# Moving a scan's multiplier into PSUM, sharing two accumulator banks, and moving a norm into the scan

## What is computed

```
delta = softplus(x_trans @ W1 + b1)                  # 128 channels per token
Bm, Cm = x_trans @ W2 + b2, x_trans @ W3 + b3        # 16 states per token
dA    = exp(-celu(delta[..., None] * A))             # A is 128 x 16
h_new = dA * h_prev + x_trans[..., None] * delta[..., None] * Bm
output = einsum('bln,bldn->bld', Cm, h_new)          # summed over the 16 states
```

## Time and profile before

| | us |
|---|---|
| median of 3 runs | 293.52 |
| the 3 runs | 293.46, 293.52, 296.5 |
| the profiled execution | 293.67 |
| its span | 292.0 |
| PE, DVE, ACT, POOL busy | 234.0, 249.1, 178.7, 137.4 |

### The profile page before, as it was taken

The page is one execution under the profiler, slowest core; times in us unless marked ns, Lnnn a source line. Parts: engine busy times, 40 slices in busy tenths (PEclk is TensorE's granted clock), DMA queues, the critical chain, the costliest instruction groups (busy, mean ns, idle before and its releaser), DMA issues.

```text
span 292.0 us, 2594 instructions
## 1 busy us (share of the span) xinstructions
PE 234.0 (80%) x825; PEld 152.2 (52%) x825; DVE 249.1 (85%) x358; ACT 178.7 (61%) x234; POOL 137.4 (47%) x89
## 2 busy tenths in 40 slices
PE   0837767987997476985997887959899999999980
PEld 0836435633664143442453343417688877888860
DVE  4996999999998999999999998578995459799465
ACT  3566874669779967687697875275533365083320
POOL 2360795000006246999778974203873328435310
PEclk9977999999999659799898997999999999999997
DMA  6920000000000000000000000000000000020002
GB/s 181 396 97 1 3 0 0 0 0 0 2 0 0 0 0 1 0 0 3 0 0 0 0 1 0 0 2 2 0 2 0 0 0 3 0 72 2 0 0 72
DMA packets 3822, 6.15 MB, mean 21 GB/s; under 512 B 384, under 2 KB 2656, under 8 KB 3552
## 3 DMA queue, kind: packets, MB, share of 16 engines
q1 hardware_dynamic: 3808, 5.97, 6.0%
HBM read 4.92 MB, written 1.05 MB: 20 GB/s over the span
## 4 chain that ended last, share of the span: by engine, by line
DVE 48%; PE 38%; issue 8%; ACT 3%; DMA 1%; DVEq 0%; ACTq 0%
PE ps L1084 12%; PE ps L1085 12%; DVE bs L804 6%; DVE bx L804 4%; DVE bs L798 4%; PE ps L1036 4%; PE ps L1055 3%; DVE x1r L725 3%; DVE bx L798 3%; DVE bs L835 2%; PE ps L935 2%; DVE tr L725 2%; DVE xr L850 2%; DVE x1r L723 2%; DVE low_max L714 1%
## 5 line engine op out<-in xcount | busy, mean ns | idle before, releaser
L577 ACT ACTIVATE bs<-ps,vec 128x512 f32<-128x512 f32 x48 | 32.5, 690 | 37.2 <-PE ps L1085 36.0
L1036 PE MATMUL ps<-tr,h0sel 96*128 96x512 f32 x64 | 22.7, 479 | 13.0 <-DVE bx L804 7.1
L1055 PE MATMUL ps<-bs,centre 128*128 128x512 f32 x52 | 28.5, 689 | 0.0
L396 POOL TENSOR_TENSOR xr<-bs,xr 128x512 fp32r<-128x512 f32 x12 | 15.9, 1331 | 26.7 <-DVE xr L850 26.7
L354 POOL TENSOR_TENSOR bdl<-bs 128x512 f32<-128x512 f32 x4 | 5.1, 1282 | 47.2 <-DVE bs L771 47.2
L1036 PEld LDWEIGHTS ps<-tr,h0sel 96*128 96x128 f32 x64 | 12.2, 206 | 28.1 <-DVE bs L804 13.4
L1084 PE MATMUL ps<-xr,wf 128*128 128x512 f32 x64 | 25.2, 393 | 0.0
L798 DVE SCALAR_TENSOR_TENSOR bs<-bdl,amax,bs 128x1024 f32<-128x1024 f32 x14 | 25.1, 1825 | 0.0
L1085 PE MATMUL ps<-xr,wf 128*128 128x512 f32 x64 | 25.1, 391 | 0.0
L545 ACT ACTIVATE bs<-bs 128x2048 f32<-128x2048 f32 x9 | 17.2, 1906 | 9.7 <-DVE bs L798 7.0
L804 DVE TENSOR_TENSOR bs<-bs,ps 128x2048 f32<-128x2048 f32 x9 | 20.5, 2280 | 0.9 <-PE ps L1036 0.9
(11 more groups left out here) (219 smaller groups left out, 682.2 us busy)
## 6 DMA issues: line engine op xcount, KB each, us to landing
bs<-in_w_mlp_dram SPq DMA_DIRECT2D x2, 1024.0 KB, 9.6
bx<-in_x_dram SPq DMA_DIRECT2D x4, 256.0 KB, 4.6
out_dram<-bdl SPq DMA_DIRECT2D x4, 256.0 KB, 2.3
bx<-in_w_mlp_dram SPq DMA_DIRECT2D x1, 768.0 KB, 6.7
bdl<-in_w_ssm_dram SPq DMA_DIRECT2D x1, 448.0 KB, 9.3
wa<-in_w_attn_dram SPq DMA_DIRECT2D x1, 256.0 KB, 2.8
w0raw<-in_w_ffn_dram SPq DMA_DIRECT2D x1, 192.0 KB, 8.6
h0T<-in_state_dram SPq DMA_DIRECT2D x1, 48.0 KB, 8.8
```

What stands on the lines that cost most here:

```text
L396: g.tensor_tensor(sl[:, 1, o, :], hbuf[k][:, o, :], full(sl[:, 0, o, :]), ALU.subtract).then_inc(m_lo_p, 1)
L577: a.activation(hbuf[k][:, o, :], ps[:, mbank(i, stage, k, o) % RING, :], ACT.Gelu if stage else ACT.Silu, scale=vec[:, s + o:s + o + 1]).t ...
L1036: last = m.matmul(ps[:, 2 * j + k, :], h0sel[:, n, :], tr[0:96, 0, cs(2 * (e // NG) + k)], start=True, stop=True)
L1055: last = m.matmul(ps[:, 4 + 2 * (e // NG) + k, :], centre[:, :], vbuf[e % NB][:, j, k * CH:(k + 1) * CH], start=False, stop=(e % NG == NG ...
```

## The change

What it does:

1. delta of the running pair is kept also in PSUM banks 6 and 7 (`delta_ps`), and `state_v` reads it there. DVE writes it for the first pair with two sums of 128 x 512, and for the second pair with one copy of 128 x 1024 in pass 7.
2. Both pairs accumulate in banks 4 and 5. The second pair's `state_first` waits for the first pair's norm, so the sums of passes 8 to 11 are taken later than before; the buffers are 7 instead of 5 for that (two more lie in the unused tile of the x splits). The feed-forward layer's ring of banks becomes 0, 1, 2, 3, 6, 7.
3. The first pair's norm is inside the scan: squares and copies in pass 10, variance in pass 10, ln and exp in pass 11, products and splits in passes 12 and 13. The second pair's stays behind the scan, with three tiles of the feed-forward layer's products ahead of its variance.
4. The beginning: ACT moves C and B out of PSUM unrounded (`c_and_b`), POOL rounds C and takes its low part (`c_parts`), DVE copies B and multiplies (`c_times_b`), DVE instead of POOL adds up delta of the first pair, the exponents of pass 0 come ahead of the logarithms of chunks 2 and 3.
5. POOL takes one `state_v` in passes 3, 5, 6, 7, 9, 10, 11, 13 and 14 (9, before 7).

```diff
-        vbuf = [b[:, :].rearrange("p (k n) -> p k n", k=GN) for b in (bx1, bx2, bs1, bs2, bs3)]
+        vbuf = [b.rearrange("p (k n) -> p k n", k=GN)
+                for b in (bx1[:, :], bx2[:, :], x1_f32[:, 0, 2:], x1_f32[:, 1, 2:], bs1[:, :],
+                          bs2[:, :], bs3[:, :])]
+        D_BANK = (6, 7, 4, 5)
+        delta_ps = ps[:, 6:8, :]
...
-            return e % 2 == 1 and e > 1 and j == 1
+            return e % 4 != 0 and 2 < e < NE - 1 and j == 1
...
+            def c_parts(c):
+                pool.wait_ge(c_full, c + 1)
+                g.tensor_copy(tr[0:96, 0, cs(c)], bs3[0:96, cs(c)]).then_inc(c_hi, 1)
+                pool.wait_ge(c_hi, c + 1)
+                g.tensor_tensor(tr[32:64, 0, cs(c)], bs3[32:64, cs(c)], full(tr[32:64, 0, cs(c)]),
+                                ALU.subtract).then_inc(c_lo, 1)
...
+            c_parts(0)
+            c_parts(1)
+            pool.wait_ge(d_ok0, 2)
+            gain_of(0)
+            gain_of(1)
+            c_parts(2)
+            c_parts(3)
...
             for e in range(NE):
                 if e + 1 < NE:
                     state_t(e + 1)
                 state_da(e)
+                if e < 2:
+                    log_part(2 + e)
                 if e == NG + 2:
+                    y3_square(0)
+                    y3_square(1)
+                if e == NG + 3:
+                    y3_rstd(0)
+                    y3_rstd(1)
...
+                        tile = vbuf[e % NB][:, j, :].rearrange("p (k n) -> p k n", n=CH)
+                        v.scalar_tensor_tensor(tile, delta_ps, amax[:, n:n + 1], tile, ALU.mult,
+                                               ALU.add).then_inc(e_v, 1)
...
+            def x3(c):
+                dve.wait_ge(y3_rs, c + 1)
+                v.tensor_tensor(bxt[:, cs(c)], bxt[:, cs(c)], bdl[:, cs(c)], ALU.mult).then_inc(x3_ok, 1)
+                split(x3_ok, x3_hi, x3_lo, bxt, lambda c: parts(lr, c), c)
...
             for e in range(NE):
+                if e + 1 == NG:
+                    delta_of_second_pair()
                 if e + 1 < NE:
                     state_v(e + 1)
                 state_p(e)
                 if e in (0, 1):
-                    direct(2 + e)
+                    direct(2 * e)
+                    direct(2 * e + 1)
+                if e == NG + 2:
+                    y3_copy(0)
+                    y3_copy(1)
+                if e in (NG + 4, NG + 5):
+                    x3(e - NG - 4)
...
+                if 1 <= e <= NG or e > NG + 4:
                     state_sum(e - 1)
+                if e == NG + 2:
+                    y3_variance(0)
+                    y3_variance(1)
+                if e == NG + 3:
+                    state_first(2)
+                    state_first(3)
+                    state_sum(NG)
+                    state_sum(NG + 1)
+                if e == NG + 4:
+                    state_sum(NG + 2)
+                    state_sum(NG + 3)
```

More of the change, by code:

```diff
@@ L237, in build, with ring @@
         PAIR = 6 * KH
-        RING = 6
+        RING_BANKS = (0, 1, 2, 3, 6, 7)
+        RING = len(RING_BANKS)
+        OUT_BANK = 4
+        def ring(b):
+            return ps[:, RING_BANKS[b % RING], :]
         def mtile(i, stage, k, o):
@@ L373, in _ @@
             r = 0
-            for e in range(1, NE, 2):
+            for e in range(1, NE):
                 if r < len(on_pool) and on_pool[r][0] == e:
@@ L552, in _ @@
                 state_da(e)
+                if e < 2:
+                    log_part(2 + e)
                 if e == NG + 2:
[L554 to L562, removed]
+                    y3_square(0)
[3 more added lines that the diff above has]
+                    y3_rstd(1)
+            y3_square(2)
+            y3_square(3)
+            y3_rstd(2)
+            y3_rstd(3)
             def norm_sd(i, k):
@@ L824, in _ @@
             v.tensor_tensor(b[:, 0, :], b[:, 0, :], b[:, 1, :], ALU.add).then_inc(e_add_last, 1)
-            for c in range(NCH):
-                dve.wait_ge(y3_rs, c + 1)
-                v.tensor_tensor(bx2[:, cs(c)], ps[:, 4 + c, :], bx2[:, cs(c)], ALU.mult).then_inc(x3_ok, 1)
-                split(x3_ok, x3_hi, x3_lo, bx2, lambda c: parts(lr, c), c)
+            y3_copy(2)
+            y3_copy(3)
+            x3(2)
+            x3(3)
             def mlp_tiles(i, stage, k):
@@ L1017, in _ @@
             pe.wait_ge(f1_ok, NCH)
-            m.matmul(ps[:, 7, 0:NLOW], ones[:, :], low_max[:, :], start=True, stop=True).then_inc(low_mm, 1)
+            m.matmul(ps[:, 5, 0:NLOW], ones[:, :], low_max[:, :], start=True, stop=True).then_inc(low_mm, 1)
             for c in range(NCH):
@@ L1088, in product, with gated @@
                 return last
-            def gated(low_weights, i, k):
+            def gated(low_weights, i, k, tiles):
                 wait_split(pe, x3_lo, 2 * i + k)
-                for o in range(KH):
+                for o in tiles:
                     wo = slice(o * P, (o + 1) * P)
@@ L1097, in gated @@
                         wait_bank(pe, b)
-                        if b < 4:
-                            pe.wait_ge(y3_ln, b + 1)
-                        elif b < RING:
-                            pe.wait_ge(x3_ok, b - 3)
-                        last = product(low_weights, ps[:, b % RING, :], f, wo, parts(lr, 2 * i + k))
+                        last = product(low_weights, ring(b), f, wo, parts(lr, 2 * i + k))
                     last.then_inc(mlp_mm, 1)
@@ L1112, in hidden @@
                             wait_low(pe, mtile(i, stage - 1, k, kk))
-                        last = product(low_weights, ps[:, b % RING, :], 3 + (stage - 1) * KH + kk,
+                        last = product(low_weights, ring(b), 3 + (stage - 1) * KH + kk,
                                        slice(o * P, (o + 1) * P), (src[:, 0, kk, :], src[:, 1, kk, :]),
```

236 lines of the change are left out of this document (140 added, 96 removed).

## The result

The changed kernel takes 300.87 us (median of four runs, 300.49 to 301.30) where the kernel before takes 293.72 beside it. The ratio is 1.022, with a 95% interval of 1.016 to 1.029. A second comparison gave 300.51 us and 1.018 (1.014 to 1.022). It is slower, as forecast, but by 5 to 7 us instead of 3, and 300.87 lies above the range of 288.0 to 299.5. The kernel before has medians of 293.7 to 296.0 us in the four comparisons of this document, so a kernel's time is read by its ratio to the kernel before on the same chip.

The account below looks back on a forecast made before the run. It took DVE as the bound, its `state_v` taking turns with POOL. From 293.67 us it added 2.3 in the scan, took off 0.7 behind it and added 1.2 for the clock: 296.5, range 288.0 to 299.5.

Parts of the forecast that it names:

- the clock: TensorE at its 1.2 GHz level after idling, in passes 1 and 2: 1.2 us slower, bounds 0 and 2.5.
- delta in PSUM: `state_v` in the scan takes 1.2 us start to start, free of turns; DVE needs 63 us instead of 80.
- Rival D: `state_v` on PSUM still takes turns with POOL, 14 us more on DVE: 305 us, chance 0.03.
- The beginning: Up to the end of pass 0's `state_p`: DVE waits 6.3 us in turns with POOL, E(0) 0.7 later.
- rival A: No turns at the start nor in the norm, POOL's small operations fit DVE's gaps: 287.7 us, chance 0.20.
- rival B: Turns of DVE and POOL at the scan's start count only half: 293.6 us, chance 0.15.
- Passes 3 to 11: PE spaces passes 4, 5, 8, 9 by 3.63 us; POOL's shares put E(6), E(10) 9.0 after E(4), E(8).
- The norm inside: Passes 11 to 15: ACT's norm work, then DVE's norm operations taking 6.6 us instead of 1.8; E(15) 2.3 later.
- Rival C: A second low-clock stretch around pass 10 delays variance, ln and exp by 1.6 us: 299.4 us, chance 0.18.
- Behind the scan: From E(15) to the first product on the gates: 0.7 us saved including the ramp, bounds 0 and 2.8.
- the ramp: Behind the scan, the three tiles that lie ready give perhaps 0.3 us more.

Follow-up runs that it names:

- the other execution: The changed kernel run once more without edits, on the chip of the later variants: 300.51 us, ratio 1.018 to the kernel before.
- The early reductions: Changed kernel with the first pair's norm products and splits behind the scan, plus that norm's reductions one pass earlier: 292.24 us, ratio 0.990.
- products behind the scan: Changed kernel with the first pair's norm products, roundings and low parts moved behind the last `state_p`: 296.21 us, ratio 1.002.
- both (early and odd): Changed kernel with norm products behind the scan, norm reductions a pass earlier, and POOL's shares on odd passes as before the change: 292.21 us, ratio 0.990.
- shares on odd passes: Changed kernel with norm products behind the scan, plus POOL's `state_v` shares on odd passes as in the kernel before: 293.55 us, ratio 0.994.
- both, PE kept busy: Kernel with early norm reductions and odd-pass POOL shares, plus zero-weight matmuls, seven behind `b_times_c(1)` and one behind `b_times_c(3)`: 293.08 us, ratio 0.995.
- B and C from PSUM: Changed kernel with B and C at the scan's beginning read from PSUM by ACT and DVE as before the change: 303.40 us, ratio 1.025.

## Why the prediction was wrong

The mechanisms were right, and the sum was too small: one term, the clock, was sized for one place and came in three. The account follows E(e), the end of `state_p` of pass e.

**delta in PSUM**: 1.27 us each, 1.2 from start to start, no turns. As forecast, and shown by taking it back (7 us). Rival D fell.

**The beginning**: E(0) 109.57, forecast 111.1. The turns are there, so rival A fell, but DVE waits 4.5 us in them, not 6.3: the last pairs of operations found POOL done, since it had waited for ACT by then. That is 1.5 in the change's favour, less than rival B's half (3.2). In the other execution all of it stands 1.09 later and takes equally long.

**Passes 3 to 11**: E(3) to E(5) 8.0 for 7.3, then 11.3, 7.5 and 11.25 for 11.1, 7.3 and 11.1. The two waits for POOL's shares are where they were put.

**The norm inside**: E(12) to E(13) is 9.3 for 10.0. The product, rounding and low part take 5.9 for 6.6. E(13) to E(15) is 10.0 for 9.8.

**The step that failed is the clock.** The prediction says "bounds 0 and 2.5, I take 1.2", for passes 1 and 2 alone. The traces show three places:

- E(0) to E(3) took 17.4 instead of 15.0. All of it is DVE's wait of 2.37 for PE, which from `state_ch(2)` to `state_ch(3)` takes 7.7 us. The same kinds of work mostly at clock 1.00 (165.06 to 170.65) take 5.6, so 2.1 of the 2.37 is the clock by these rows.
- E(11) to E(12) took 7.4 instead of 5.7. ACT waits 1.35 and 0.36 us for the variance, which takes 3.62 at 0.50 and 1.88 at 1.00 (behind the scan, at 200.41). Rival C had this at 1.6, with a chance of 0.18; it is the case that came nearest, with 299.4. The early reductions, which keep the clock up there, are in line with it, but they move other things too.
- Behind pass 14, the sum takes 5.29 instead of 3.60, for a third stretch that no case of the prediction had. Work for PE ahead of it brought 3.60 back, and 0.6 us of the time. The run with delta in SBUF agrees: PE is idle there for 1.43 us instead of 3.46, the sum takes 3.60 without any added work, and the first product on the gates stands 14.2 behind E(15), too.

No run held the clock up through the first place. But ten traces have the same work there (the one with delta in SBUF is left out, DVE itself is later in it), and the clock came back sooner in some than in others, mostly by itself:

| trace | mean granted clock | `state_ch(2)` to `state_ch(3)`, us | DVE's wait in pass 3, us |
|---|---|---|---|
| products behind the scan | 0.61 | 7.91 | 2.59 |
| changed, the second execution | 0.62 | 7.75 | 2.44 |
| changed | 0.63 | 7.69 | 2.37 |
| both (early and odd) | 0.68 | 7.17 | 1.85 |
| shares on odd passes | 0.70 | 6.94 | 1.63 |
| both, PE kept busy | 0.74 | 6.66 | 1.34 |
| B and C from PSUM | 0.75 | 6.51 | 1.26 |

The other three lie among the first rows: 7.86 and 2.55, 7.84 and 2.51, 7.70 and 2.39. (In two of the ten the profile puts the wait down to ACT, but names the exponent of pass 4, for which this `state_p` does not wait.) Where the clock is higher PE's work is shorter, and the wait shrinks by the same amount to 0.1 us. Down to 1.26 that is measured; that it goes on to 0.3 at full clock is an estimate from the 5.6.

Together that is about 4.4 us instead of 1.2. The bound of 2.5 was one for one stretch, and it was taken for the whole term. Two things in hand spoke against it: the trace of the kernel before has the low clock in at least four places and not only in that of the earlier trace rows, and the prediction's own times (9.0 from E(8) to E(10)) leave PE idle in pass 10. Between E(3) and E(5) 0.7 more is lost, but not to the clock: it is 1.00 there, and PE, still behind, has a sum of eight and a `state_ch` one behind the other.

**Behind the scan** it takes 14.8 from E(15) to the first product on the gates, forecast 12.6. After E(15), with the forecast in brackets, the held back sum ends at 2.6 (0.9), the tiles begin at 5.6 (4.3) and end at 8.8 (7.1), the exponents end at 12.4 (10.8). So the 1.7 us of the slow sum run through the whole chain. But without them it is still 14.2: when the sum takes 3.60, PE is idle for 0.83 ahead of the tiles (0.81 with delta in SBUF), and the profile shows nothing that it waits for. So some 1.0 is a late start of the tiles that the prediction didn't have and whose cause is open. The rest is 0.3 for DVE's order, in which product, rounding and low part of both chunks, 2 x 1.8, stand ahead of the first gate, and the 0.3 that the prediction expected at the ramp. From the first product to the end it takes 94.05, against 94.3 before.

The sum, in us: 1.5 and 0.7 less for the beginning and the norm; 2.4 + 0.7 + 1.7 + 0.7 more in the scan (the last for small differences in four intervals); 2.2 more behind it, and 0.3 less to the end. That is 5.2, less the 1.2 that stood for the clock: 4.0, which is 300.49 - 296.5. The 2.2 us of turns that did not come hid part of the miss, and that was luck.

So the change gains about 7 us on `state_v` and loses more: 4 to 6 in turns of the norm's products, 2 to 3 in the order of POOL's shares (with an overlap), and over 4 in TensorE's clock, against some 0.5 in the kernel before. Without the first, and with the norm's reductions a pass earlier, it is 1% faster than the kernel before by the runs.

## What to carry to other kernels

Where a change takes load off the engine that is the bound, list the places in which TensorE ends the wait, one by one, and give each a range from the 1.2 to the 2.4 GHz level, that is up to twice the time of its matmuls; a bound for one place is no bound for the term. The length of the idle time alone did not tell here: the clock fell behind 1.76, 1.82, 3.46 and 3.57 us of it, and stayed at 1.00 behind the same 1.82 in the run with B and C from PSUM and behind 1.95 with the early reductions. So read the granted clock of the kernel before all along the path first. Work that reads SBUF twice on VectorE belongs where GpSimd is silent or where VectorE waits anyway; moving six operations from inside the scan to behind it gave back 4 to 6 us. A share for GpSimd is placed by what it stands behind on its own queue, and two edits that remove waits at the same pass add up only in part (3.3 and 3.7 us alone, 4.9 together).

## What was unexpected of the hardware

- The granted clock fell to 0.50 again within 5 us of 7 us of back to back matmuls on zeros (102.9 to 109.8 us), with no idle time over 1.3 us in between, on small and part-filled matmuls (32 and 96 rows). After 9.2 us of them it fell as well, from 118 to 120.
- The clock came back at different moments in executions whose programs are equal up to there: DVE's wait in pass 3 was 1.63, 1.85, 2.37, 2.39, 2.44 or 2.59 us.
- A sum sped up by 1.7 us brought 0.6 at the work that waits for it; 0.83 us of idle time came up behind it for which the profile names no cause.
- In turns even the shortest operation waits for a whole one of the other engine: a rounding of 0.43 took 2.49 beside a POOL sum of 2.75 us.
